# Attention with transposed probabilities one step later: the lag of the transposes from three to four steps

## The reference

```python
q = (hidden_states @ Wq).reshape(b, s, HEADS, HEAD_DIM)     # 16 heads of 64; k, v alike
q, k = _apply_rotary(q, sin, cos), _apply_rotary(k, sin, cos)
logits = jnp.where(causal, jnp.einsum('bhqd,bhkd->bhqk', q, k), MASK_VAL) / 8
out = jnp.einsum('bhqk,bhkd->bhqd', jax.nn.softmax(logits, axis=-1), v)
...
x = x + _layernorm(attn(_layernorm(x)) @ Wo)
scores = H * softmax(einsum('bsd,hd->bsh', _layernorm(x), Wr) + br)
x = x + _layernorm(2 * einsum('bshr,hor,bsh->bso', low, B, scores))
```

## Time and profile before

| | us |
|---|---|
| median of 3 runs (1069.79 to 1070.48) | 1069.91 |
| profiled execution, device time | 1069.58 |
| its span, from the first to the last instruction | 1067.8 |
| PE busy | 1049.9 |
| DVE busy | 756.9 |
| ACT busy | 591.3 |
| POOL busy | 439.4 |

### The profile page before, as it was taken

How to read it: one execution, slowest core, us unless ns; L and a number is a source line. 1 busy time by engine, 2 the same in 40 slices (tenths; PEclk the granted TensorE clock), 3 DMA queues, 4 the chain that set the end, 5 groups by cost and what they waited for, 6 DMA issues and landing times.

```text
span 1067.8 us, 20069 instructions
## 1 busy us (share of the span) xinstructions
PE 1049.9 (98%) x5559; PEld 871.3 (82%) x5559; DVE 756.9 (71%) x2138; ACT 591.3 (55%) x1390; POOL 439.4 (41%) x422
## 2 busy tenths in 40 slices
PE   7999999999999999999999999999999999999996
PEld 6888888888888888888888888888877888888884
DVE  8777777776666666666666666666766877777777
ACT  7556666666555665565555655555576333333334
POOL 4153443435353635444452625344457232333221
PEclk9999999999999999999999999999999999999999
DMA  7022324241311256021111112020333323322311
GB/s 280 36 84 70 128 69 128 74 129 55 104 51 34 95 182 227 10 71 33 52 49 31 52 29 69 10 69 17 87 132 93 108 88 107 118 99 87 109 61 60
DMA packets 58663, 90.36 MB, mean 85 GB/s; under 512 B 3568, under 2 KB 36336, under 8 KB 58608
## 3 DMA queue, kind: packets, MB, share of 16 engines
q1 hardware_dynamic: 58464, 89.44, 25.9%
q10 hardware_dynamic: 144, 0.26, 0.1%
HBM read 64.52 MB, written 25.17 MB: 84 GB/s over the span
## 4 chain that ended last, share of the span: by engine, by line
PE 90%; DVE 3%; issue 2%; ACT 2%; POOL 0%; DVEq 0%; ACTq 0%; POOLq 0%
PE bank L1472 46%; PE bank L1403 25%; PE bank L1499 6%; PE bank L1518 3%; PE bank L1517 3%; PE bank L1633 2%; PE bank L1610 1%; PE bank L1445 1%; PE bank L1634 1%; PE bank L1520 1%; PE bank L1433 1%; ACT prob L740 1%; DVE prob L1053 0%; DVE k_hh L1092 0%; PE bank L1415 0%
## 5 line engine op out<-in xcount | busy, mean ns | idle before, releaser
L595 POOL TENSOR_SCALAR prob<-prob,rinv 128x128 f32<-128x128 f32 (+3 forms) x256 | 150.5, 588 | 436.8 <-DVE rinv L1063 436.8
L1472 PE MATMUL bank<-big_hi,w_hi 128*128 128x512 f32 (+1 forms) x776 | 329.4, 424 | 0.3 <-DVE big_lo L1034 0.3
L740 ACT ACTIVATE prob<-prob,nmax 128x128 f32<-128x128 f32 (+3 forms) x256 | 144.0, 562 | 304.3 <-DVE nmax L1053 302.7
L1472 PE MATMUL bank<-big_hi,w_lo 128*128 128x512 f32 (+1 forms) x776 | 304.5, 392 | 0.0
L1472 PE MATMUL bank<-big_lo,w_hi 128*128 128x512 f32 (+1 forms) x776 | 302.1, 389 | 0.0
L1472 PEld LDWEIGHTS bank<-big_hi,w_lo 128*128 128x128 f32 x776 | 145.6, 188 | 33.2
L1071 DVE TENSOR_TENSOR pT_lo<-bank,pT_hi 128x128 fp32r<-128x128 f32 (+3 forms) x256 | 123.7, 483 | 56.0 <-ACT pT_hi L751 53.3
L1472 PEld LDWEIGHTS bank<-big_hi,w_hi 128*128 128x128 f32 x776 | 146.6, 189 | 16.5 <-issue 0.4
L1472 PEld LDWEIGHTS bank<-big_lo,w_hi 128*128 128x128 f32 x776 | 147.1, 190 | 11.6
L1063 DVE RECIPROCAL rinv<-rsum 128x1 f32<-128x1 f32 x256 | 40.8, 159 | 129.3 <-ACT prob L740 128.9
L1053 DVE CUSTOM_DVE_ANT_0 prob<-bank,mask 128x128 f32<-128x128 f32 (+3 forms) x256 | 124.1, 485 | 9.2 <-PE bank L1403 5.1
(11 more groups left out here) (146 smaller groups left out, 1927.7 us busy)
## 6 DMA issues: line engine op xcount, KB each, us to landing
w_raw<-in_wqkv SPq DMA_DIRECT2D x48, 512.0 KB, 4.4
attention_out<-o_sum SPq DMA_DIRECT2D x64, 128.0 KB, 2.3
w_raw<-attention_out SPq DMA_DIRECT2D x16, 512.0 KB, 4.8
land<-in_x SPq DMA_DIRECT2D x16, 512.0 KB, 3.7
out<-res SPq DMA_DIRECT2D x14, 512.0 KB, 2.6
xin<-in_x SPq DMA_DIRECT2D x12, 512.0 KB, 5.7
xT_hold_hi<-xin SPq DMA_DIRECT2D x8, 512.0 KB, 3.6
xT_hold_lo<-xn SPq DMA_DIRECT2D x8, 512.0 KB, 5.4
```

Of the source, the lines that this page charges most:

```text
L595: pool.tensor_scalar(p, p, rinv[:, q % 4:q % 4 + 1], 1.0, ALU.mult, ALU.mult).then_inc(prob_done, 1)
L740: act.activation(prob[:, q % 4, 0:n], prob[:, q % 4, 0:n], ACT.Exp, scale=-1.0, bias=nmax[:, q % 4:q % 4 + 1], accum_out=rsum[:, q % 4:q % ...
L1472: done = pe.matmul(grp_ps[(b + k) % 2][:, cols], w, xt[:, cols], start=at == 0, stop=at == GROUP_MM - 1)
```

## The change

A constant `TURN_LAG = 4` takes the place of the 3 in `turn_probs` on PE, `pt_high` on ACT and `pt_low` on DVE: probabilities are transposed three steps after their scores, where it was two. The weighted sums move from the ends of steps 0 and 4 to the ends of steps 1 and 5 (in slot 33 the second ones from step 3 to step 4), `o_lower` from steps 1 and 5 to 2 and 6, and `o_add` from steps 1 and 6, ahead of `invert`, to steps 2 and 6, behind `pt_low`. In slot 33 the last `o_lower` and `o_add` stay in step 3. No instruction is added or removed.

```diff
--- before.py
+++ after.py
@@ -62,6 +62,7 @@
 AHEAD = EARLY // 2
 PART = KC // 2
 HOLD_AT = (4, 7)
+TURN_LAG = 4
 X_BANKS = (4, 5, 6, 7, 2, 3)
 
 
@@ -742,7 +743,7 @@
                                    ).then_inc(exp_done, 1)
 
             def pt_high(u, s):
-                a, q, g = trailing(u, s, 3)
+                a, q, g = trailing(u, s, TURN_LAG)
                 if real(a):
                     i, h = q % QT, q // QT
                     act.wait_ge(t_done, g + 1)
@@ -808,9 +809,9 @@
                     exponent(u, s)
                     if s == 0 and real(u - 1):
                         v_raw(u - 1, 1 - b)
-                    if s == 1 and real(u - 2):
+                    if s == 2 and real(u - 2):
                         o_lower(u - 2, 0)
-                    if s == 5 and real(u - 2) and not (isinstance(u, int) and u > UNITS):
+                    if s == 6 and real(u - 2) and not (isinstance(u, int) and u > UNITS):
                         o_lower(u - 2, 1)
                     if s == 2 and real(u - 1):
                         v_high(u - 1, 1 - b, fill)
@@ -1134,10 +1135,6 @@
                         if s in (3, 6):
                             rotate(u, b, s // 6)
                     closing = isinstance(u, int) and u >= UNITS
-                    if s == 1 and real(u - 2) and not closing:
-                        o_add(u - 2, 0)
-                    if s == 6 and real(u - 2) and not (closing and u > UNITS):
-                        o_add(u - 2, 1)
                     leads = ahead or (isinstance(u, int) and u == UNITS - 1)
                     if leads and s == 7:
                         k_low(u, b, 0)
@@ -1149,8 +1146,10 @@
                     pt_low(u, s)
                     if s == 0 and not closing and real(u - 1):
                         k_low(u - 1, 1 - b, 1)
-                    if closing and s == 1 and real(u - 2):
+                    if s == 2 and real(u - 2):
                         o_add(u - 2, 0)
+                    if s == 6 and real(u - 2) and not (closing and u > UNITS):
+                        o_add(u - 2, 1)
                     if real(u):
                         if s in (4, 5):
                             q_low(u, b, s - 4)
@@ -1565,9 +1564,9 @@
                     project_third(1)
                     turn_probs(u, s)
                     project_third(2)
-                    if s == 0:
+                    if s == 1:
                         attend(u - 2, b, 0)
-                    if s == (3 if isinstance(u, int) and u == UNITS + 1 else 4):
+                    if s == (4 if isinstance(u, int) and u == UNITS + 1 else 5):
                         attend(u - 2, b, 1)
                     for c in x_chunks(u, s):
                         x_chunk(1, c)
```

## The result

The changed kernel takes 1110.9 us (median of 4 runs, 1107.8 to 1112.2) against 1070.0 before: 1.0377 times as long, 95% interval 1.0355 to 1.0399. Its profiled execution took 1110.85 us with a span of 1109.1, 41.3 more than before. The forecast was 1102, the range 1077 to 1114.

A forecast was written before the change was run, and what follows sets the result against it. PE, busy 98%, was taken as the bound, with a DVE, ACT and POOL ring as long behind it. Steady odd slots +24.6, early pairs +4.9, slot 1 +3 and end 0 made +32.5: 1102 us, range 1077 to 1114.

The forecast's parts named there:

- up to slot 1's end: Slot 1, which has the order of the steady stage, loses like an odd slot: +3 us.
- slots 2 to 9: Four early pairs, at 51.7 us a pair against 50.5: +4.9 us together.
- slots 10 to 29: Ten odd slots from 11 to 29, with a pair at 50.9 us instead of 48.44: +24.6 us together.
- behind them, to the end: Last slots: old waits go, a new one before the last weighted sums comes; 0, from -1.5 to +1.5 us.
- The term of step 7: Step 7 of an odd slot: POOL's subtraction gets ahead of K's copy; about 6.1 us instead of 4.0, +2.1.
- The pair: An even and an odd slot of the steady stage together on DVE: from 48.25 to about 50.9 us.
- the ring: DVE, ACT and POOL handing each other work in fixed order: 48.25 us a pair, under PE's 48.32, growing to about 50.9.
- rival 1: K's copy keeps its place ahead of POOL's subtraction: about 48.8 us a pair, +9, 1079 us; chance 0.13.
- The new wait before the last weighted sums: Last slot: the last weighted sums wait for transposes, ACT and DVE in a row, some 1.75 us.
- the wait of 1.00 at 795.57: PE's wait near the end, 1.17 us from start to start, claimed to go with the change.
- rival 3: Nothing to measure: the ring lengthens by what the waits at the transposes give back; 1068 to 1071 us; chance 0.03.
- rival 2: Faster: the ring stays under 48.32 us a pair, PE's waits for probabilities go; about 1067 us; chance 0.07.

The follow-up runs named there:

- the one with one column: The changed kernel with POOL's subtraction for K's next weights cut to one of its 1024 columns: 1082.26 us, 1.0117 times before.
- K first: The changed kernel with K's low half and its copy ahead of the reciprocal in step 7 of every slot: 1073.75 us, 1.0039 times before.

## Why the prediction was right, and where it was off

**The mechanism** held in each of its links: the 512-wide tile in step 7, the late start of K's low half behind it, the subtraction that gets in, and on PE an odd slot that grows and an even one that doesn't. Taking the subtraction away took 28.6 us away, the falls of the clock with it. One link differs by an instruction: it is K's low half that stands still, and not the copy as at 311, because it starts 0.17 us after the subtraction instead of 0.30 before it. Two readings were loose by 0.3 us, and no term hangs on them: the subtraction at 604.23 begins 0.31 before the copy ends, not after it, and the copy at 312.17 ends 0.29 after POOL.

**The terms,** each measured as the delay against before of the first product of a slot's step 2. (The first scores of a slot won't do: the change puts them ahead of the weighted sums of 1.2 us that stood ahead of them before.)

| term | forecast | measured |
|---|---|---|
| up to slot 1's end | +3 | +3.3 |
| slots 2 to 9 | +4.9 | +1.2 |
| slots 10 to 29 | +24.6 | +27.1 |
| behind them, to the end | 0 | +2.8 |
| falls of the clock (estimate) | not there | +6.8 |
| sum | +32.5 | +41.2 |

The measured terms are without the falls. Slot 10's product, for one, comes 6.23 us late, slot 30's 38.12, and 4.8 of the difference are the fall at 323 and the part of that at 784 up to there: 27.1. That the total is only 9 us low is in part luck: one term was 3.7 too high, the others together 12.4 too low.

**The term of step 7** (+2.1) was right: 51.1 - 49.0 = 2.1 between the changed kernel and the one with one column. **The pair** was forecast at 50.9 and is 51.1. The split was a little off: the negations stand 27.12 and 23.98 apart, for 27.3 and 23.5. In the even slot PE sets the pace: the chain that ended last runs over PE alone from 631.39 to 660, K's copy in step 7 is 0.45 us early, and so PE's 24.17 counts. The forecast named that limit (24.16), but its pair of 50.9 has the ring's 23.5 in it. The pair without the collision, 48.8 in rival 1, is 49.0.

**Slots 2 to 9** were charged 1.2 a pair and cost 0.3. The mis-sized term is the walk through their steps: 4.9 would have been near for the moved sums and joins alone (4.3 measured), but together with the lag they cost 1.2 (the lag alone costs 0.2 there). Which of the charged steps the lag gives back was not tried.

**The end** was put at 0 as a balance of two sides. The new wait before the last weighted sums was forecast at 1.75 and is 1.46 (1.73 from start to start); that the wait of 1.00 at 795.57 goes was right too. What was missing are three waits before transposes in the last two slots, 2.0 us together, for the low part of tiles. The longest:

```profile
847.00 0.41 PE L1498 MATMUL bank<-ident,prob 128*128 128x128 f32 x2 [0.87 <-DVE pT_lo L1072]
```

The forecast dealt only with what stands behind the last transposes, not with the steps ahead of them, where the 512-wide tile now lies as well.

**The falls of the clock** are the largest miss. The sum took a standstill of PE at its own length. Three of them cost more than that, by up to 6.8 us. In all profiled runs here each fall within the attention (twelve in six kernels) stands at a wait of PE of 2.35 to 3.37 us; the six kernels whose longest wait there is 1.46 us or less, once PE's work has begun, have none.

**What would show it:** the wait for k_hh (30.2, at 14 places), eleven instances over 2 us of K's low half (L1091 before, L1092 now) and the share of PE (96%, for about 95) came as written. Two points did not. The waits for POOL's probabilities shrank from 6.0 to 2.4, they didn't go. And PE's busy time rose by 9.5 us; the slow stretches account for up to 6.8 of it.

**The rivals.** Rival 1, 1079 with K's copy in its place, is nearly what the one-column kernel gives (1082.3): the same case, made by hand. The changed kernel with K first would be at about 1071 without the 2.8 us that it loses behind slot 31, which is rival 3; the time of rival 2 was reached by no kernel with the lag of four. That the extra step relieves PE at the probabilities is true, and those waits were 0.6% of its time.

## What to carry to other kernels

When an engine at 98% hides a second ring of the same length, walk that ring step by step: moving a wide tile by one step adds no work on PE and can change who asks first for something shared. An instruction that is held up appears as a longer instruction, not as a wait, so compare the longest instance of a line with its usual one. And put short work that others wait for into a place where its engine waits anyway: one line did that here, and gained 0.24% before the change and 37 of the 41 us after it.

## What the runs showed of the hardware

Cutting POOL's subtraction into two instructions didn't free DVE: the engines took turns, so that K's low half waited for the first half (1.68 us), POOL's second half for the low half (1.72), and the copy for that (1.39). A low half that reads PSUM and one tile of SBUF (pT_lo, 0.69 us, in the run with K's low half ahead of it) ran unhindered beside the same subtraction, one that reads two tiles of SBUF (K's, 2.79 for 0.67) did not. Nor did the copy of K's high half, which reads one tile of SBUF and writes it back to SBUF (2.57 for 0.42, 1.39 beside the subtraction in two halves).

At a wait of 2.4 to 3.4 us on an otherwise busy PE a stretch of 3.4 or 6.8 us at a granted clock of 0.50 can begin, in which 512-column matmuls start 0.43 us apart instead of 0.23. It doesn't always: of the eleven waits behind K's held low half in the changed kernel the two longest (3.37 and 2.88 us) and the shortest (2.39) came with a fall, the eight between them (2.43 to 2.56) did not. What decides was not settled, and it seems to make the time of this kernel less steady: the one run of four with a mean clock of 0.995 instead of 0.990 to 0.992 took 1107.8 us, the others 1110.9 to 1112.2.
